# Start addresses in SBUF of the float32 operands of TensorE: probabilities, normalised features, features of layer 1, inputs and identity

## The reference

```
def _L0_gnn_ref(x, adj, weight, bias):
    support = jnp.einsum('bni,io->bno', x, weight)
    return jnp.einsum('bnm,bmo->bno', adj, support) + bias

def _L1_gnn_ref(feats, adj_mat, fc_w, fc_b, q_w, q_b, k_w, k_b, fp_w, fp_b):
    feat_proj = (feats @ fc_w + fc_b).reshape(bs, n, HEADS, dim).transpose(0, 2, 1, 3)   # 8 heads
    q = feat_proj @ q_w + q_b
    k = feat_proj @ k_w + k_b
    logits = q + jnp.swapaxes(k, -1, -2)
    masked = logits + (1.0 - adj_mat[:, None]) * NEG
    masked = jax.nn.leaky_relu(masked, negative_slope=0.01)
    attn = jax.nn.softmax(masked, axis=-1)
    out = (attn @ feat_proj).transpose(0, 2, 1, 3).reshape(bs, n, HEADS * dim)
    return jax.nn.sigmoid(out @ fp_w + fp_b + feats)

h = jnp.maximum(_layernorm(x, axis=-1), 0.0);  x = x + _L0_gnn_ref(h, adj, ...)
h = jnp.maximum(_layernorm(x, axis=-1), 0.0);  x = x + _L1_gnn_ref(h, adj, ...)
```

## Time and profile before

| | |
|---|---|
| time, median of 3 runs | 1406.91 us (1406.39 to 1406.93) |
| the profiled execution: time, span | 1406.65 us, 1404.9 us |
| TensorE busy (matmuls) | 1394.7 us, 99% |
| TensorE's loads of stationary operands | 1252.5 us, 89% |
| VectorE busy | 1285.1 us, 91% |
| ScalarE busy | 1126.5 us, 80% |
| GpSimd busy | 1102.0 us, 78% |
| DMA, mean rate | 89 GB/s |

### The profile page before, as it was taken

How to read it: one execution, slowest core, us unless ns; L and a number is a source line. 1 busy time by engine, 2 the same in 40 slices (tenths; PEclk the granted TensorE clock), 3 DMA queues, 4 the chain that set the end, 5 groups by cost and what they waited for, 6 DMA issues and landing times.

```text
span 1404.9 us, 31603 instructions
## 1 busy us (share of the span) xinstructions
PE 1394.7 (99%) x9048; PEld 1252.5 (89%) x9048; DVE 1285.1 (91%) x4408; ACT 1126.5 (80%) x3429; POOL 1102.0 (78%) x1295
## 2 busy tenths in 40 slices
PE   9999999999999999999999999999999999999998
PEld 7898899899899889998998898998989989988987
DVE  7999999999999999999999999999999999998996
ACT  4878788788888888887888888888878878887876
POOL 4788878878778878778787788787787887888764
PEclk9999999999999999999999999999999999999999
DMA  7423323323223233233232232232332322322221
GB/s 238 98 63 107 107 54 106 91 69 106 71 88 106 55 105 106 54 105 97 63 106 80 79 106 61 99 106 54 105 103 58 106 88 73 106 67 85 77 61 41
DMA packets 177132, 124.69 MB, mean 89 GB/s; under 512 B 137808, under 2 KB 143568, under 8 KB 177104
## 3 DMA queue, kind: packets, MB, share of 16 engines
q1 hardware_dynamic: 176816, 124.35, 30.3%
q10 hardware_dynamic: 288, 0.01, 0.0%
HBM read 105.98 MB, written 18.35 MB: 89 GB/s over the span
## 4 chain that ended last, share of the span: by engine, by line
PE 94%; POOL 2%; issue 1%; DVE 1%; DMA 1%; ACT 0%; POOLq 0%; SPq 0%; ACTq 0%; DVEq 0%
PE gbank L381 48%; PE ybank L381 24%; PE tbank L481 8%; PE bank L381 6%; PE bank L426 4%; PE bank L462 2%; PE bank L449 2%; DMA late<-key_rows 0%; POOL att L1561 0%; POOL att L1554 0%; DMA qk<-qk_w_dram 0%; DVE att L829 0%; POOL xb L1544 0%; POOL t_pos L1546 0%; POOL ends L1577 0%
## 5 line engine op out<-in xcount | busy, mean ns | idle before, releaser
L1233 ACT ACTIVATE att<-att 128x128 f32<-128x128 f32 x1024 | 397.8, 393 | 47.0 <-DVE att L836 44.0
L381 PE MATMUL gbank<-m_hi,hT_lo 128*128 128x512 f32 x1024 | 426.7, 417 | 0.0
L1554 POOL TENSOR_TENSOR att<-late,t_pos 128x512 f32<-128x512 f32 x256 | 330.6, 1293 | 120.5 <-PE tbank L481 115.8
L381 PE MATMUL gbank<-m_hi,hT_hi 128*128 128x512 f32 x1024 | 403.2, 394 | 0.0
L381 PE MATMUL gbank<-m_lo,hT_hi 128*128 128x512 f32 x1024 | 401.3, 392 | 0.0
L812 DVE TENSOR_TENSOR g_lo<-gbank,g_hi 128x512 fp32r<-128x512 f32 x512 | 341.4, 678 | 47.1 <-ACT g_hi L1226 42.0
L1561 POOL TENSOR_TENSOR att<-att,rinv 128x512 f32<-128x512 f32 x256 | 289.4, 1131 | 107.1 <-DVE rinv L841 106.5
L1226 ACT ACTIVATE g_hi<-gbank 128x512 fp32r<-128x512 f32 x512 | 291.1, 595 | 39.6 <-PE gbank L381 39.4
L829 DVE TENSOR_SCALAR_CACHE_REDUCE att<-att,qs 128x128 f32<-128x128 f32 x1024 | 291.6, 341 | 27.0 <-POOL att L1554 26.7
L381 PE MATMUL ybank<-g_hi,pT_hi 128*128 128x256 f32 x1016 | 281.5, 277 | 0.0
L381 PE MATMUL ybank<-g_hi,pT_lo 128*128 128x256 f32 x1016 | 281.4, 277 | 0.0
(11 more groups left out here) (97 smaller groups left out, 2323.1 us busy)
## 6 DMA issues: line engine op xcount, KB each, us to landing
late<-key_rows SPq DMA_DIRECT2D x64, 1024.0 KB, 6.1
g_in<-graph_dram SPq DMA_DIRECT2D x64, 512.0 KB, 3.4
out_dram<-ends SPq DMA_DIRECT2D x63, 256.0 KB, 3.9
qs<-key_rows SPq DMA_DIRECT2D x128, 4.0 KB, 2.5
key_rows<-kq_sb SPq DMA_DIRECT2D x64, 24.0 KB, 1.4
att<-fc_wT_dram SPq DMA_DIRECT2D x4, 256.0 KB, 5.6
late<-fp_w_dram SPq DMA_DIRECT2D x4, 256.0 KB, 5.3
ends<-fp_w_dram SPq DMA_DIRECT2D x2, 512.0 KB, 7.9
```

The lines of the kernel that those rows point to most:

```text
L381: mm = pe.matmul(out_ap, w, m, start=first and n == 0, stop=last and n == len(terms) - 1)
L1233: e = act.activation(a[:, s], a[:, s], ACT.Exp, scale=-1.0, bias=a[:, CH + h:CH + h + 1], accum_out=esum[j][c][:, h:h + 1])
L1554: gp.tensor_tensor(a, keys[q][:, j, c * HC:(c + 1) * HC, :], t_pos[q][:, j, :].unsqueeze(1).broadcast_to([P, HC, P]), ALU.add)\
```

## The change

Only the allocation of tiles changes. `h0_f`, `h1` and `att_all` are allocated among the tiles that begin on multiples of 256 bytes, ahead of `fcb`. `ident` and `g_in` are allocated in the group that begins 64 bytes beyond. A part of the probabilities now takes 512 + 128 numbers, 2560 bytes, instead of 2064, of which the first 516 are used as before. The steps of all engines and their order are the same.

Counted from the sizes, the start addresses in bytes beyond a multiple of 256:

| tile | before | after |
|---|---|---|
| `h0_f`, `h1` (each of the three) | 32 | 0 |
| `att`, parts (0,0), (0,1), (1,0), (1,1) | 96, 112, 128, 144 | 0, 0, 0, 0 |
| `g_in`, and the transposed adjacency in it | 32 | 64 |
| `ident` | 64 | 64 |
| `ah`, `hT`, `pT` | 0 | 0 |
| `w0`, `m`, `g`, `u` | 64 | 64 (22,528 bytes higher) |

```diff
--- before.py
+++ after.py
@@ -78,15 +78,18 @@
         pT_hi, pT_lo = two("pT_hi", [P, H, P], F32R, SPAN), two("pT_lo", [P, H, P], F32R, SPAN)
 
 
+        h0_f, h1 = three("h0_f", [P, J, D], F32, SPAN), three("h1", [P, J, D], F32, SPAN)
+        att_all = sb("att", [P, J * NC * CH + J * NC * P], F32, SPAN)
         fcb = sb("fcb", [P, H * DT], F32, SPAN)
         w0_hi, w0_lo = sb("w0_hi", [P, DT, D], F32R, LINE), sb("w0_lo", [P, DT, D], F32R, LINE)
         m_hi, m_lo = sb("m_hi", [P, DT, H * D], F32R, LINE), sb("m_lo", [P, DT, H * D], F32R, LINE)
         g_hi, g_lo = two("g_hi", [P, H * D], F32R, LINE), two("g_lo", [P, H * D], F32R, LINE)
 
         u = sb("u", [P, DT, 2 * HALF], F32R, LINE)
-
-
-        ident = sb("ident", [P, P])
+        ident = sb("ident", [P, P], F32, LINE)
+        g_in = three("g_in", [P, J * (D + 2 * P)], F32, LINE)
+
+
         b0_row = sb("b0_row", [P, D])
         none = sb("none", [P, DT, 2 * HALF])
         qk = sb("qk", [P, DT, 2])
@@ -100,10 +103,8 @@
         gate = sb("gate", [P, 2 * U])
 
 
-        g_in = three("g_in", [P, J * (D + 2 * P)])
-        h0_f, xb = three("h0_f", [P, J, D]), three("xb", [P, J, D])
+        xb = three("xb", [P, J, D])
         t_pos = three("t_pos", [P, J, P])
-        h1 = three("h1", [P, J, D])
         x1 = three("x1", [P, J, D])
         feats_b = three("feats", [P, J, D])
         st0, mv0, rs0 = three("st0", [P, J, 6]), three("mv0", [P, J, 2]), three("rs0", [P, J])
@@ -120,8 +121,7 @@
         late = sb("late", [P, U * KEYS * P + H * DT])
         keys = [late[:, k * KEYS * P:(k + 1) * KEYS * P].rearrange("p (j h n) -> p j h n", j=J, h=H) for k in range(U)]
         qs = three("qs", [P, J, H])
-        att_all = sb("att", [P, J * NC * (CH + HC)])
-        att = [[att_all[:, n * (CH + HC):(n + 1) * (CH + HC)] for n in range(NC * j, NC * (j + 1))] for j in range(J)]
+        att = [[att_all[:, n * (CH + P):n * (CH + P) + CH + HC] for n in range(NC * j, NC * (j + 1))] for j in range(J)]
         esum = [two(f"esum{j}", [P, HC]) for j in range(J)]
         rinv = [two(f"rinv{j}", [P, HC]) for j in range(J)]
         ends = sb("ends", [P, 4 * J * D + H * DT])
```

## The result

The changed kernel takes 1414.81 us (median of 4 runs, 1414.54 to 1415.08) against 1406.65 us (1406.14 to 1406.93) of the kernel before in the same session: ratio 1.0058, 95% interval 1.0041 to 1.0076. That is 8.2 us slower. The prediction, 1405.6 us with a range to 1408.8, is wrong in sign and outside its range. Nothing about the kind of bound changed.

What follows compares the result with a forecast made beforehand. TensorE alone was taken to bound the kernel; -0.01 behind blocks and -0.01 in the aggregation made -0.02 us a pair, x 64 = -1.3 us, so 1405.35, plus 0.26 for the median: 1405.6 us, range 1402.0 to 1408.8.

Steps and rivals of the forecast that it cites:

- What bounds the kernel: Middle of the run: TensorE alone, busy for 99% of the span; one pair of graphs takes 21.43 us, 64 pairs.
- Direct effects: Per pair: -0.01 us behind the transposition blocks and -0.01 us in the aggregation, together -0.02 us.
- only 3.09 us of the 21.43 can change directly: Per pair, only 20 transposes and 8 aggregation records get another alignment: 0.44 x 5 + 0.89 us.
- own signs of being wrong: Wrong in kind: TensorE waits in the loop, or project or attend changes distance; in size: pair moves over 0.05 us.
- a stagger worth 10 ns: Products behind transposition blocks: stationary loads and products take a few products to settle; 0.01 us a pair taken as gain.
- Rival A: Around the blocks: the stagger goes, -0.09 us a pair, 5.8 us, 1401.1 us; 29% from its half on.
- Rival B: Whole kernel: nothing happens, 1406.9 us, as old starts are all multiples of 16; 20% for changes within 0.5 us.
- Rival C: Transposes and aggregation slow to the distance of attend: 0.085 us a pair, 5.4 us, 1412.3 us; 13% with smaller losses.
- its own signs: Chain in the middle: 0.45 us in a transposition block and 0.91 us in the aggregation.
- Rival D: m, g, w0 and u lie 22,528 bytes higher; 1% of their streaming would be 10 us, either way; 4%.
- seven tenths of the chain: Share of TensorE's chain in which m, g, w0 and u stream; 1% of that would be 10 us.
- The range: Whole run, 8 in 10: from 1402.0 us, leaving out the full gain of Rival A, to 1408.8 us, into Rival C's lower half.

Runs made afterwards that it cites:

- e7: Kernel before with the first product of project 5 issued twice, no address changed: 1422.42 against 1406.27 us, ratio 1.0115.
- e6: Kernel before with only g_in moved, 64 bytes beyond 256 in place of 32: 1407.06 us, ratio 1.0002.
- e9: Kernel before with the parts of the probabilities 2560 bytes apart, at their old starts beyond 256: 1406.94 against 1406.59 us, ratio 1.0002.
- e1: Kernel before with m, g, w0, u and the identity 22,528 bytes higher, every alignment as before: 1406.66 against 1406.27 us, ratio 1.0001.
- e2: Kernel before with every new alignment of the change, tiles left where they were to within 416 bytes: 1414.99 against 1406.27 us, ratio 1.0062.
- e3: Kernel before with only the probabilities realigned, on 256 bytes and 2560 bytes apart: 1414.84 against 1406.27 us, ratio 1.0061.
- e4: Kernel before with only h1 on 256 bytes: median 1412.09 us of 10 runs in two groups, ratio 1.0026.
- e5: Kernel before with only h0_f on 256 bytes: 1409.85 against 1406.86 us, ratio 1.0021.
- e10: Kernel before with probability parts 2560 bytes apart and only part (0,0) on 256 bytes, the others at their old starts: 1416.74 us, ratio 1.0073.
- e12: Kernel before with u alone on 256 bytes; w0, m and g keep their place modulo 256: 1422.45 us, ratio 1.0114.
- e18: Kernel before with parts 2560 bytes apart, part (1,0) and h0_f on 256 bytes, other parts at old starts: 1410.38 us, ratio 1.0025.
- e14: Kernel before with w0, m, g, u and the identity 192 bytes beyond 256 in place of 64; its time is not in the text.
- e17: Kernel before with w0, m, g, u and the identity 32 bytes beyond 256 in place of 64: 1425.4 us.
- e13: Kernel before with w0, m, g, u and the identity 128 bytes beyond 256 in place of 64: a pair of 21,873 ns.
- e15: Changed kernel with w0, m, g, u, the identity and g_in 128 bytes beyond 256 in place of 64: 1433.31 us, ratio 1.0186.
- e11: Kernel before with w0, m, g, u and the identity on 256 bytes, 64 lower: 119.3 ns a 256-column product; its time is not in the text.
- e16: Kernel before with w0, m, g, u and the identity 96 bytes beyond 256 in place of 64: 1437.0 us.

## Why the prediction was wrong

- **What bounds the kernel** was right: TensorE alone, without waits, before and after.
- **Direct effects** were small, as forecast: -0.02 us a pair forecast, and -0.009 is what is left beside the slow blocks. The aggregation gave 3 ns where I took 10, and transposes stay at 0.44 us. That the sign agrees says little, since e7 has the same 3 ns without a change of address.
- **The step that failed** is "only 3.09 us of the 21.43 can change directly" as a stand-in for all that can change. The sum priced each edited block by itself and held "attend" at 1.36 and "transform" at 1.37. The 6.8 us of a pair in those blocks have two lengths, 52 ns apart, and the edited blocks ahead choose between them. That term, +155 ns a pair, is seventeen times the rest, with the other sign. The prediction's own signs of being wrong were "attend" changing its distance and a pair moving by more than 0.05 us; both came, with 113.3 to 118 ns and 0.146 us.
- **The rows were there.** The prediction looked at one window in the middle. The chain of the kernel before in its opening, where the loop isn't in step yet, has both lengths at the same addresses:

```profile
75.94 1.42 PE ybank L381 x12
...
83.82 1.42 PE bank L381 x12
...
89.81 1.42 PE ybank L381 x12
...
121.71 1.36 PE ybank L381 x12
```

  I took the 1.37, 1.38 and 1.39 behind blocks in the earlier trace rows for a stagger worth 10 ns. It is a sign of a phase that is carried on, and the question to ask was what else hangs on it.
- **Rival A** (nothing left behind the blocks, 1401.1) did not occur: project still takes 1.37 to 1.39. **Rival B** (nothing) is how g_in's new place alone (e6) and the new distance of the parts alone (e9) come out, but it isn't the time. The Trainium skill (SBUF — State Buffer, Specifications (TRN2)) charges by the crossing of 16-byte lines, and by that no start in this study should matter; the measured 1406.7, 1425.4 and 1437.0 us at 64, 32 and 96, all multiples of 16, say otherwise of the moving operands. **Rival C** had the sign and, by coincidence, nearly the time (1412.3), by the wrong mechanism: blocks stay at 0.44 and the aggregation at 0.89, so its own signs are absent. **Rival D** named a row that moved (1.36), but its cause, the shift, is excluded by e1. Its "seven tenths of the chain" is too low: project, attend and transform are 17.9 of the 21.43 us, over eight tenths, so 1% is 11 us.
- **The range** was built from direct effects, with 12% on slower. The kernel before has all five blocks at the fast pace, so of this term it could only lose: of the eleven ways to disturb it at moving operands of 64 without adding work (after, e1 to e6, e9, e10, e12, e18) eight were 3 to 16 us slower, three the same, none faster.

## What to carry to other kernels

When one engine runs without a wait, the start times of its instructions, by block and in ns, are the profile to read. A kernel that has equal blocks of two lengths anywhere in its trace may be thrown from one to the other by a change of 3 ns some blocks ahead of them, as e5 was. Before pricing a neutral-looking edit, look in the opening of the trace, where the rhythm is broken, for how slow the same blocks can be, and put that beside the forecast as a rival. Compare versions by the whole repeated turn, and run more executions of one that lies between two times.

## What the runs showed of the hardware

- Float32r products of 256 moving columns with 128 stationary ones, in a row, at full clock: 113.3 or 117.8 to 118.0 ns for moving operands at 64 bytes beyond 256 and stationary on 256 (before, after); 114 or 118 at 192 (e14); 117, in one block of the turn 118, at 32 (e17); 118.5 to 120.4 at 128 (e13, e15); 119.3 at 0 (e11) and 120 at 96 (e16). For 512 columns 229 ns in the mean at 64, about 3 more at 32, 96, 128 and 192 (2878 to 2882 ns for 12 against 2845), 1 less at 0.
- Float32 transposes of 128 columns start 108 to 110 ns apart inside a block at every place tried, except that the first distance is 115 in one block of the turn in some kernels (before, e3, e5, e7).
- The pace lasts the block of 12. At 64 it follows the last distance before it: 226 or 229 gives 118, 231 or 232 gives 113. At 192, 233 and 236 go with 114, 231 with 118.
- The same program settled in two rhythms on the same chip, 1406.6 to 1407.5 and 1411.8 to 1412.9 us (e4).
- Open: what makes the round of three and the two paces; it is observed, not explained. Only the moving operands were moved, never the stationary ones of these products, so whether the place itself or its distance from the stationary operand counts wasn't told apart. Whether accesses of the other engines take part wasn't tested; that the marker held in the opening as in the loop (203 of 206 blocks) speaks against it. That e4's two groups are two phases is argued from their distance; only the upper was profiled. The last distance is a marker of the phase, and whether it or something that goes with it decides was not told apart.
